# Attention: second half of a group's value products moved into the next step, keys copied by ScalarE

## The reference

```python
H = 16
HD = D // H
qkv = x @ w_attn
q, k, v = jnp.split(qkv, 3, axis=2)
...
att = jnp.einsum('bhqd,bhkd->bhqk', q, k) * (1.0 / math.sqrt(HD))
causal = jnp.tril(jnp.ones((Tc, Tc), dtype=bool))
att = jnp.where(causal[None, None], att, -jnp.inf)
att = jax.nn.softmax(att, axis=-1)
y = jnp.einsum('bhqk,bhkd->bhqd', att, v)
y = y.transpose(0, 2, 1, 3).reshape(Bc, Tc, Dc)
return y @ w_proj
```

## Time and profile before

| what | value |
|---|---|
| median of three runs | 1908.45 us (1907.8 to 1911.01) |
| the profiled execution, own time | 1903.04 us |
| its span, first to last instruction | 1901.3 us |
| attention, 1498 to 1693 us of the span | 195 us |
| PE busy in the span | 1685.1 us (89%) |
| DVE, ACT, POOL busy | 1175.4 (62%), 904.9 (48%), 604.7 us (32%) |
| mean granted TensorE clock | 0.932 of full speed |

### The profile page before, as it was taken

The page is one execution under the profiler, slowest core; times in us unless marked ns, Lnnn a source line. Parts: engine busy times, 40 slices in busy tenths (PEclk is TensorE's granted clock), DMA queues, the critical chain, the costliest instruction groups (busy, mean ns, idle before and its releaser), DMA issues. The chain is left out here.

```text
span 1901.3 us, 31207 instructions
## 1 busy us (share of the span) xinstructions
PE 1685.1 (89%) x9564; PEld 1236.2 (65%) x9564; DVE 1175.4 (62%) x2691; ACT 904.9 (48%) x2397; POOL 604.7 (32%) x877
## 2 busy tenths in 40 slices
PE   2689999989999998999999999998689799977775
PEld 2367778777786776877778677787555455554553
DVE  4568677676876867768687686874444354523223
ACT  0555756647566575665756557561211133421110
POOL 0514434354342543425434254340200112213003
PEclk7899999999999999999999999996889877877998
DMA  1110010110101001010010101100011440003112
GB/s 34 41 37 14 26 39 7 33 21 21 38 7 34 15 25 40 7 33 16 25 38 7 34 13 26 22 7 10 1 34 33 185 177 1 1 1 125 42 37 80
DMA packets 121043, 65.96 MB, mean 35 GB/s; under 512 B 91424, under 2 KB 111776, under 8 KB 120864
## 3 DMA queue, kind: packets, MB, share of 16 engines
q1 hardware_dynamic: 118768, 59.28, 11.0%
q0 software_dynamic: 1536, 4.20, 0.7%
q10 hardware_dynamic: 560, 0.28, 0.1%
HBM read 46.16 MB, written 17.56 MB: 34 GB/s over the span
## 5 line engine op out<-in xcount | busy, mean ns | idle before, releaser
L857 DVE SCALAR_TENSOR_TENSOR dr_acc<-dr_raw,dr_wh,dr_acc 128x512 f32<-128x512 f32 x384 | 306.6, 812 | 64.7 <-ACT dr_acc L722 62.0
L1078 PE MATMUL dr_pp<-xnT,dr_wh 128*128 128x512 f32 x512 | 251.6, 626 | 22.2 <-issue 15.7
L1078 PEld LDWEIGHTS dr_pp<-xnT,dr_wh 128*128 128x128 f32 x512 | 95.8, 200 | 112.4 <-issue 96.5
L681 POOL TENSOR_TENSOR dr_dT<-dr_dT,cst 128x512 f32<-128x512 f32 x64 | 88.4, 1381 | 239.2 <-DVE dr_dT L891 239.2
L667 POOL TENSOR_TENSOR dr_gm<-cst,dr_hs 128x512 f32<-128x512 f32 x64 | 77.7, 1224 | 258.6 <-PE dr_pG L1118 133.2
L1151 PEld LDWEIGHTS dr_pI<-dr_Y,dr_nl 128*64 128x64 f32 (+1 forms) x1536 | 130.9, 161 | 33.8 <-issue 26.6
L1166 PEld LDWEIGHTS dr_pI<-dr_V,dr_X 128*64 128x64 f32 (+1 forms) x1536 | 130.0, 160 | 28.8 <-issue 23.7
L1151 PE MATMUL dr_pI<-dr_Y,dr_nl 128*64 128x64 f32 (+1 forms) x1536 | 139.9, 247 | 4.7 <-DMA dr_Y<-dr_blocks_y 3.0
L1166 PE MATMUL dr_pI<-dr_V,dr_X 128*64 128x64 f32 (+1 forms) x1536 | 139.6, 247 | 1.0 <-DVE dr_V L981 0.8
L721 ACT ACTIVATE dr_raw<-dr_pp 128x512 f32<-128x512 f32 x128 | 76.3, 596 | 132.5 <-PE dr_pp L1078 123.8
L1110 PE MATMUL dr_pp<-dr_wh,xnT 128*128 128x256 f32 x512 | 122.8, 383 | 14.6 <-ACT dr_acc L722 14.6
(11 more groups left out here) (262 smaller groups left out, 3752.6 us busy)
## 6 DMA issues: line engine op xcount, KB each, us to landing
dr_wh<-in_w_head SPq DMA_DIRECT2D x16, 776.0 KB, 4.7
ex_w<-in_moe SPq DMA_DIRECT2D x18, 608.0 KB, 15.7
dr_wo<-in_w_out SPq DMA_DIRECT2D x16, 256.0 KB, 4.8
dr_sorted_x<-ex_zero SPq DMA_DIRECT2D x1, 3968.0 KB, 27.4
dr_sorted_y<-so_xt SPq DMA_DIRECT2D x31, 128.0 KB, 1.7
m_w<-in_moe SPq DMA_DIRECT2D x8, 384.0 KB, 3.1
so_xt<-dr_sorted_x SPq DMA_DIRECT2D x3, 1024.0 KB, 10.2
dr_blocks_l<-dr_nl SPq DMA_DIRECT2D x128, 16.0 KB, 1.7
```

The costliest lines, as they stand in the source:

```text
L681: pool.tensor_tensor(d, d, over(k.c(C_LE), 1, U), ALU.mult).then_inc(s_am, 1)
L857: dve.scalar_tensor_tensor(acc[q][:], raw[q][:, w:w + S], wh[at.ps][:, col:col + 1], acc[q][:], ALU.mult, ALU.add).then_inc(done[q], 1)
L1078: mm = pe.matmul(flat(ps), wh[at.ps][:, w0:w0 + P], k.xnT[:, kt, b * S:(b + 1) * S], start=(kt == 0), stop=(kt == KT - 1))
```

## The change

Two things change in the attention, and nothing in its arithmetic. First, the list: the second half of the value products of group n-1 leaves the end of step n (where it stood behind the projections) and enters step n+1, behind batch 1. The transposes "yb" of that group move from behind batch 0 to behind batch 2 of step n+1. `y_take` goes with the last value product, `normalise` with "yb". "yt" of the first batch element moves behind the first half of the last group's value products. Second, `k_take` is done by ACT as an Identity activation with a per-partition bias, and no longer by DVE.

```diff
--- before.py
+++ after.py
@@ -1770,26 +1770,27 @@
     order = [("v", j, 0) for j in range(NT // 2)]
     order += [("proj", which, (0, b)) for b in range(B) for which in "qk"]
     for step in range(STEPS):
-        for k in range(NBATCH + 2):
+        new, old, older = step < NG, 1 <= step <= NG, step >= 2
+        for k in range(NBATCH + 1):
             for i in range(BATCH):
-                if step < NG and k < NBATCH:
+                if new and k < NBATCH:
                     order.append(("s", step, BATCH * k + i))
-                if 1 <= step <= NG and 1 <= k <= NBATCH:
+                if old and k >= 1:
                     order.append(("w", step - 1, BATCH * (k - 1) + (i + 2) % BATCH))
-            if k == 0 and step >= 2:
+            if older and k == 1:
+                order += [("pv", step - 2, NUNIT // 2 + i) for i in range(NUNIT // 2)]
+            if older and k == 2:
                 order.append(("yb", step - 2, 0))
-            if step == NG and k == 2:
+            if old and k == 3:
+                order += [("pv", step - 1, i) for i in range(NUNIT // 2)]
+            if step == NG and k == 3:
                 order += [("yt", 0, kt) for kt in range(KT)]
-            if step == NG and k == 4:
-                order += [("pr", 0, j) for j in range(2)]
-            if k == NBATCH and step < NG:
-                order.append(("mt", step, 0))
-            if 1 <= step <= NG and k in (3, 5):
-                if k == NBATCH + 1 and step // 2 + 1 < NQ:
-                    order += [("proj", which, (step // 2 + 1, step % 2)) for which in "qk"]
-                order += [("pv", step - 1, BATCH * (k - 3) + i) for i in range(2 * BATCH)]
-        if step == 0:
-            order += [("proj", which, (1, 0)) for which in "qk"]
+        if new:
+            order.append(("mt", step, 0))
+        if step // 2 + 1 < NQ:
+            order += [("proj", which, (step // 2 + 1, step % 2)) for which in "qk"]
+        if step == NG:
+            order += [("pr", 0, j) for j in range(2)]
         if step == NG + 1:
             order += [("yt", 1, kt) for kt in range(KT)] + [("pr", 1, j) for j in range(2)]
     return order
@@ -2032,6 +2033,17 @@
                     used(act, "mt", old, 0)
                 act.activation(qT[Q % 2][:, b * S:(b + 1) * S], ps[:], ACT.Copy, scale=AD ** -0.5).then_inc(taken, 1)
 
+            def k_take(which, at):
+                Q, b = at
+                ps, taken = filled(act, "proj", which, at)
+                if Q >= 2:
+
+                    old = GROUPS.index((Q - 2, b))
+                    act.wait_ge(s_score, NUNIT * (old + 1))
+                    act.wait_ge(s_wt, NUNIT * (old + 1))
+                act.activation(kT[Q % 2][:, b * S:(b + 1) * S], ps[:], ACT.Identity,
+                               bias=mask[:, S:S + 1]).then_inc(taken, 1)
+
             def exp(g, i):
                 kb, r = UNITS_W[i]
                 u = W_AT[g, i]
@@ -2056,6 +2068,10 @@
                     v_take(a, b)
                 if kind == "proj" and a == "q":
                     q_take(a, b)
+                if kind == "proj" and a == "k":
+                    if b == (0, 0):
+                        act.wait_ge(s_mask, 16)
+                    k_take(a, b)
                 if kind == "w":
                     exp(a, b)
                 if kind == "pv" and b == NUNIT - 1:
@@ -2065,17 +2081,6 @@
 
         @block.vector
         def _(dve):
-            def k_take(which, at):
-                Q, b = at
-                ps, taken = filled(dve, "proj", which, at)
-                if Q >= 2:
-
-                    old = GROUPS.index((Q - 2, b))
-                    dve.wait_ge(s_score, NUNIT * (old + 1))
-                    dve.wait_ge(s_wt, NUNIT * (old + 1))
-                dve.tensor_scalar(kT[Q % 2][:, b * S:(b + 1) * S], ps[:], mask[:, S:S + 1], None,
-                                  ALU.add).then_inc(taken, 1)
-
             def maxi(g, i):
                 qt, r = UNITS_S[i]
                 dve.wait_ge(s_score, NUNIT * g + i + 1)
@@ -2113,8 +2118,6 @@
             dve.wait_ge(s_mask, 16)
             dve.wait_ge(s_zero, 4)
             for kind, a, b in ATTN_ORDER:
-                if kind == "proj" and a == "k":
-                    k_take(a, b)
                 if kind == "s":
                     maxi(a, b)
                 if kind == "mt":
```

## The result

The changed kernel has a median of 1916.24 us (1910.92 to 1922.51, 15 runs). The kernel before, timed beside it, has 1910.43 us (1897.54 to 1914.8, 15 runs). The ratio is 1.0040, with an interval from 1.0023 to 1.0057: 4.4 to 10.9 us slower, 7.6 us by the ratio (5.8 us between the two medians). The profiled execution took 1916.24 us.

The account below looks back on a forecast made before the run. PE was taken to bound the attention, losing its full clock in six of seven steps. Order +3.0, five falls +7.0, two falls saved -8.2 gave +1.8 us, 1910.3 us, said as 1910; range 1902 to 1918 us.

Parts of the forecast that it names:

- The step at full clock: A step with projections, batch 0 to batch 0, without clock loss: +0.60 us, 18.2 us instead of 17.58.
- the first joint: Batch 1 to 2: a value product cannot start beside the running 32-row weight product, +0.59 us per step.
- the shorter line of DVE: `normalise` no longer stands between the maxima of batch 0 and batch 1 on DVE: -0.62 us per step.
- the second joint: Batch 2 to 3: "yb" uses all 128 rows and cannot start beside a running 32-row product, +0.55 us per step.
- the cover: DVE and ACT catch up while PE drains and does value products: -0.5 us per step, between nothing and 1.2 us.
- The rival in which the drains are covered: Waits on the ring hide PE's drains: -1.3 instead of +3.0 us at full clock, 1906 us with five falls; 8%.
- The keys at nothing: Moving the keys' copy from DVE, where it was hidden, to ACT, idle then, costs and gains zero.
- A falling step at about 23 us: Steps 1 to 7: a step that loses the full clock should take about 23 us.
- The number of falls: Steps 1 to 7: five of seven lose the full clock, since a late fall would come after the moved value products.
- the falls stay: Rival: batch 1 stays thin and each fall costs more; six falls +7.3 us (1915.8), seven +12.8 us (1921.3); 25%.
- The price of a fall: Moved all-row work runs at 1.2 GHz: +1.4 us in each falling step; each fall saved gains 4.1 us.
- Seven falls for the median execution: Profiled execution, six falls, was 5.4 us faster than the median run, about one fall; so seven for the median.

Follow-up runs that it names:

- the first experiment: Kernel before with only `k_take` moved from DVE to ACT, order untouched: 1907.77 us against 1907.92 us, ratio 1.0003.
- The filler: Kernel before plus two needless 128-row matmuls in each of steps 1 to 7, behind "yb" and inside batch 1: 1895.13 us, ratio 0.9929.
- The block: Changed kernel with second half of value products, projections and "yb" together behind batch 0: 1887.2 us, ratio 0.9881 against the kernel before.
- the shorter maxima: Row maxima over the last 128 columns only; order of before 1870.64 us, of the change 1872.5, all 128-row work behind batch 0 1871.61.
- the second profile of after: The changed kernel executed and profiled once more, nothing altered: 1912.15 us.

## Why the prediction was wrong

**The step at full clock was right.** +0.60 us was forecast, 18.2 us instead of 17.58; it is 18.18. By place the terms hold to 0.1 us. Up to batch 2: the value products, the first joint and the shorter line of DVE, 0.79 + 0.59 - 0.62 = +0.76, measured +0.80 us. From batch 2 to 3: "yb" and the second joint less the cover, 0.58 + 0.55 - 0.5 = +0.63, measured +0.69. From there to the first half of the value products no term was put, and -0.10 us is measured. At the step's end -0.79, measured -0.79. The value products start 6.07 us into the step (6.0 forecast), batch 2 at 6.85 (6.8). "yb" alone gave +0.46 us by the same terms, 0.58 + 0.55 - 0.62 = +0.51 before any cover. The rival in which the drains are covered is refuted. The Trainium skill (TensorE: Matmul & The Clock Gate, Part 3) lets a weight load overlap a running matmul only if the two use different row groups; the trace agrees, the first load of a value product comes 0.76 us after the last load of batch 1, where before the change the score of batch 2 started beside the running weight product.

**The keys at nothing: right**, by the first experiment. `y_take` at nothing was not tried alone; the table by place leaves no more than 0.1 us for it.

**A falling step at about 23 us: right in size**, 23.5 us, but for another reason than the one I gave (below).

**The number of falls was wrong, and it is the step that failed.** I took five of seven, because a late fall "would come after the value products in their new place" and so "I expect it to go". That place did see none. But batch 1 ahead of it was as thin as ever, and the two steps fell earlier instead, 5.5 and 5.9 us in, before the value products at 6.07 us. Six of seven steps fell. The early fall holds about 14 us where the late one held 7, so what I had booked as falls saved became falls lengthened. I also took the piece ahead of the fall to be unchanged, since PE "had done scores and weight products only". It wasn't: the second half of the value products and "yb" had stood right before and right after batch 0 and were gone from there. In step 2 of before "yb" started at 1554.66 us, 3.6 us ahead of the fall. Moving "yb" alone was enough for the long falls, with the value products still in their old place. That this thinning is the cause is the reading that fits; it wasn't tried apart from the shift in time that comes with it. My own rival "the falls stay" said six falls, +7.3 us against a kernel with seven, that is 3.0 + 8.4 = +11.4 us against one with six; the attention shows +12.8 us. Its 1915.8 us is near the measured 1916.24 us by luck: it starts from a kernel with seven falls, which no profile shows, and what came back behind the attention wasn't in it. The filler shows what was missing from my reasoning: work on all rows inside or just ahead of the thin stretch saves falls, and here behind it saved none. The block and the shorter maxima say it from the other side.

**The price of a fall was mis-sized, both ways.** I had +1.4 us for the moved work in each falling step. In step 2, which fell early before and after, a fall costs 22.59 - 17.58 = 5.0 us before and 23.52 - 18.18 = 5.3 us after: +0.3 us, not +1.4. The clock columns tell why: the step is at 1.2 GHz for 13.6 us both times (0.70 of 22.59 us, 0.71 of 23.52 us). Work that is moved into a stretch of the same length pushes other work out of it, so the doubling that I had charged is mostly given back. But the falls of steps 3 and 4 of before, at 3.7 us, have no like in after, where steps 2, 3 and 5 each pay 5.3 to 5.4 us: +1.6 us or more for two of the falls. And 4.1 us for each late fall saved was too much from the start: a late fall of before lasts 7 us at half the clock, so it can cost 3.4 us at most. So the sum came out near the rival's although its term did not say why, which is luck again: the falls last longer, rather than the moved work being dearer. What decides whether the clock is back after 10 or after 14 us isn't settled. "yb" moved alone gave the long falls too (23.14 us, clock 0.70), with the value products where they had been.

**Seven falls for the median execution was wrong as well.** I put down the 5.4 us between the profiled execution and the median to one fall. Three profiles in the order of before, at 1903.04, 1903.67 and 1912.19 us (the last with the keys on ACT), have the same attention with six falls; the 9 us between the outer two lie ahead of it. Without this step the forecast would have been 1908.45 + 5.9 (five falls against six) = 1914.4 us, nearer in number with the same wrong count.

**How 12.8 us in the attention become 7.6 us by the ratio.** In the profiled executions 2.2 us come back behind the attention (206.50 against 208.72 us, clock 0.89 against 0.87), in the second profile of after 4.5 us (204.21 us). That leaves 8.2 to 10.6 us, inside the interval from 4.4 to 10.9. Over all thirteen profiles the part behind, in which no instruction was changed, took about 208.7 us (six times, the block among them), 206.4 (twice) or 204.2 us (five times, the value products alone and all three with short maxima among them). So it isn't tied to the changed order; what sets it was not tested.

## What to carry to other kernels

Before moving work on all rows of PE out of the way of products over 32 rows, find the stretch in which PE is thin because another engine paces it, and put the work ahead of it or into it: behind it, it came too late here to keep the clock. Price a joint between 32-row and 128-row products at its drain (here 0.55 to 0.6 us), and prefer one block to three. When a kernel loses the clock, ask of each fall how long it lasts as well as whether it comes. And when executions of one kernel differ, look in the trace for the stretch where they do before putting it down to the mechanism under study.

## What was not expected of the hardware

- PE lost its full clock without standing still for long. In the slice from 1561 us in which it fell PE is busy for 1.00 us of 1.00, with four matmul rows, and in the changed kernel's attention its longest idle time is 0.8 us. The Trainium skill (TensorE: Matmul & The Clock Gate, Why this matters for your kernels) has the clock fall through idle gaps between bursts. The trace does not agree: there was no such gap here, and what helped was two needless matmuls on all rows per step, six falls to two, 0.7% off the whole time.
- The stretch behind the attention, with the same 598 matmul rows everywhere, took 208.7, 206.5 or 204.2 us in the profiles shown, with a mean clock of 0.87, 0.89 or 0.91. A kernel's total moved by 4.5 us there without any change to that part.
- In the order of before the shorter maxima took 2.1% off the whole time, five times what the change cost, though DVE is busy for only 83 us of the attention's 174. In the thin stretch it is busy 4.30 us of 4.35, and that is where it counts.
